# The recurrent mixing layer: where VectorE adds the last batch to X and takes its moments within a step

## What is computed

```python
x = x + 0.5 * L0_ffn(layernorm(x))    # "choice": experts choose tokens
x = x + L0_attn(layernorm(x))         # "rwkv": the layer of this change
x = x + 0.5 * L0_ffn(layernorm(x))    # "choice"
x = x + 0.5 * L1_ffn(layernorm(x))    # "top2"
x = x + L1_attn(layernorm(x))         # "mlstm"
x = x + 0.5 * L1_ffn(layernorm(x))    # "top2"
```

```python
x = _layernorm(x, ln_g, ln_b)
k, v, r = (mix_n(x, last_x) @ W_n.T for n in "kvr")
den = den * td + exp(k)               # per channel, from token to token
num = num * td + exp(k) * v
out = (sigmoid(r) * num / (den + 1e-8)) @ Wo.T
```

## Time and profile before

| | |
|---|---|
| median of 3 runs | 1990.86 us (1990.62 to 1991.52) |
| the profiled execution | 1991.48 us, of which the span of the page is 1989.7 us |
| TensorE, matmuls | busy 1533.6 us (77%) |
| VectorE | busy 1483.6 us (75%) |
| ScalarE | busy 1027.4 us (52%) |
| GpSimd | busy 1048.6 us (53%) |
| the rwkv layer's reciprocals | from 391.5 to 571.4 us of the span |

### The profile page before, as it was taken

One profiled execution on the slowest core, in us unless ns is written; L12 is line 12 of the kernel. 1 busy time (PEld: TensorE's weight loads), 2 busy tenths in 40 slices (PEclk: granted clock), 3 DMA queues, 4 the chain that ended last, 5 costly groups with the idle time before them and its releaser, 6 DMA issues.

```text
span 1989.7 us, 42086 instructions
## 1 busy us (share of the span) xinstructions
PE 1533.6 (77%) x10496; PEld 1430.5 (72%) x10496; DVE 1483.6 (75%) x4465; ACT 1027.4 (52%) x2548; POOL 1048.6 (53%) x1639
## 2 busy tenths in 40 slices
PE   6399999578756999978049995469899978069993
PEld 6299999466645999977049994358888867059993
DVE  6769898688876788888627776658878877447774
ACT  2388888222314888852126663136666642036662
POOL 3527786678852355443644445405666653644442
PEclk9999999798976999996569998559999975579997
DMA  4111010370001111002122223011111100122215
GB/s 169 33 34 37 29 35 9 94 168 0 0 1 49 33 33 34 25 5 107 40 61 67 63 54 88 7 35 64 53 53 63 53 22 23 49 62 67 63 44 170
DMA packets 95551, 104.31 MB, mean 52 GB/s; under 512 B 12328, under 2 KB 75965, under 8 KB 94880
## 3 DMA queue, kind: packets, MB, share of 16 engines
q1 hardware_dynamic: 85472, 85.09, 14.5%
q0 software_dynamic: 9920, 17.35, 2.6%
HBM read 67.94 MB, written 37.97 MB: 53 GB/s over the span
## 4 chain that ended last, share of the span: by engine, by line
PE 53%; DVE 25%; issue 10%; POOL 4%; ACT 2%; DMA 2%; DVEq 1%; SPq 1%; ACTq 0%; POOLq 0%
PE banks L542 5%; PE banks L531 3%; PE banks L522 3%; PE banks L1030 3%; PE banks L524 3%; PE banks L523 3%; PE banks L1043 3%; PE banks L1032 3%; PE banks L1031 3%; DVE rwkv_over L1533 3%; PE banks L1045 3%; PE banks L1044 3%; PE banks L1065 3%; DVE bnstats L241 3%; DVE mlstm_log_decay L1961 2%
## 5 line engine op out<-in xcount | busy, mean ns | idle before, releaser
L809 POOL DMA_INDIRECT rt_y<-top_y,top_xs x182 | 178.7, 982 | 230.0 <-DVE top_y L766 207.5
L1250 DVE TENSOR_TENSOR choice_hlo<-choice_h,choice_hhi 128x512 fp32r<-128x512 f32 x256 | 172.5, 715 | 49.1 <-ACT choice_hhi L1127 48.2
L802 POOL DMA_INDIRECT rt_rows<-top_payload,top_slot x128 | 130.6, 1020 | 110.8 <-DVE top_slot L722 73.6
L1119 ACT ACTIVATE choice_h<-banks 128x512 f32<-128x512 f32 x256 | 152.3, 600 | 61.8 <-PE banks L1032 48.7
L752 DVE SCALAR_TENSOR_TENSOR top_h<-top_silu,top_xs,banks 128x176 f32<-128x176 f32 x364 | 128.5, 394 | 41.4 <-ACT top_silu L596 40.4
L1030 PE MATMUL banks<-choice_xin_hi,ec_w_hi 128*128 128x256 f32 x512 | 146.7, 287 | 6.1 <-ACT choice_xin_lo L1112 4.7
L1043 PE MATMUL banks<-choice_hhi,ec_w_hi 128*128 128x256 f32 x512 | 145.7, 285 | 2.9 <-DVE choice_hlo L1250 2.9
L1127 ACT ACTIVATE choice_hhi<-choice_h 128x512 fp32r<-128x512 f32 x256 | 146.6, 625 | 0.0
L1032 PE MATMUL banks<-choice_xin_hi,ec_w_lo 128*128 128x256 f32 x512 | 144.8, 283 | 0.0
L1031 PE MATMUL banks<-choice_xin_lo,ec_w_hi 128*128 128x256 f32 x512 | 144.7, 283 | 0.0
L1045 PE MATMUL banks<-choice_hhi,ec_w_lo 128*128 128x256 f32 x512 | 143.3, 280 | 0.0
(11 more groups left out here) (303 smaller groups left out, 5676.7 us busy)
## 6 DMA issues: line engine op xcount, KB each, us to landing
choice_token_row<-choice_tokens SPq DMA_DIRECT2D x64, 256.0 KB, 3.1
mlstm_run_row<-mlstm_run SPq DMA_DIRECT2D x32, 512.0 KB, 3.6
rt_rows<-rt_blank SPq DMA_DIRECT2D x2, 6188.0 KB, 35.8
top_xs<-rt_rows SPq DMA_DIRECT2D x182, 68.0 KB, 1.8
top_y_in<-rt_y SPq DMA_DIRECT2D x16, 512.0 KB, 7.2
X<-in_x SPq DMA_DIRECT2D x8, 512.0 KB, 6.8
ec_stage<-in_ec_w SPq DMA_DIRECT2D x2, 2048.0 KB, 15.6
out_x<-X SPq DMA_DIRECT2D x8, 512.0 KB, 7.4
```

The costliest lines, as they stand in the source:

```text
L809: pool.indirect_dma_start(d.y[self.run], bass.IndirectOffsetOnAxis(ap=at, axis=0), self.y[:, u % self.YR, :], None, bounds_check=NT * P - ...
L1250: dve.tensor_tensor(flat(self.hlo), self.h[:, c, :], flat(self.hhi).bitcast(F32), ALU.subtract).then_inc(self.hlo_done, 1)
```

## The change

VectorE's order in a step of the rwkv layer. The addition to X for batch s-1 moves from the end of the step to the place between num and under. The moments for batch s-1 (before: of batch s-2, at the beginning of the step) are parted: the statistics, with their two waits, stand between under and the reciprocal; the aggregation, with its wait, between the reciprocal and z. In step 32, which has no `mix`, addition and moments of batch 31 follow each other. Nothing else is touched: the same instructions on the same tiles and buffers, the same semaphores and counts.

```diff
+    def stats_of(self, dve, layer, b, u):
+        if inside(b):
+            n = layer * B + b
+            apart(dve, self.sh.x_done, n - B + 1, self.sh.passed)
+            self.spread(dve, n, 1, b, slice(0, TP), u)
+
+    def gather_of(self, dve, layer, b, u):
+        if inside(b):
+            self.gather(dve, layer * B + b, 1, slice(0, TP), u)
+
...
     def take(self, dve, n, count, b, tiles, u):
-
+        self.spread(dve, n, count, b, tiles, u)
+        self.gather(dve, n, count, tiles, u)
+
+    def spread(self, dve, n, count, b, tiles, u):
         apart(dve, self.scaled, n - count, self.sh.passed)
         for t in range(tiles.stop):
             i = dve.bn_stats(self.st[:, u, t, :], self.sh.X[:, bass.ds(TP * b + t, 1), :])
         i.then_inc(self.stats, count)
+
+    def gather(self, dve, n, count, tiles, u):
         apart(dve, self.stats, n + count, self.sh.passed)
         for t in range(tiles.stop):
             i = dve.bn_aggr(self.mv[:, u, t, :], self.st[:, u, t, :])
...
         def mix(b, u):
+            last = lambda part: part(dve, self.layer + 1, b - 1, 1 - u)
             td = self.td[:, 0:1].to_broadcast([P, T])
...
             dve.tensor_tensor_scan(self.num[:, u, :], td, self.ekv[:, u, :], 0.0, ALU.mult, ALU.add).then_inc(self.scans_done, 1)
+            if inside(b - 1):
+                update(b - 1, 1 - u)
             dve.wait_ge(self.scans_done, b + 1)
             dve.wait_ge(self.er1_done, b + 1)
 
             dve.scalar_tensor_tensor(out=self.under[:, u, :], in0=self.den[:, u, :], scalar=1e-8, in1=self.er1[:, u, :],
                                      op0=ALU.add, op1=ALU.mult).then_inc(self.under_done, 1)
+            last(sh.moments.stats_of)
             dve.wait_ge(self.under_done, b + 1)
             dve.reciprocal(self.over[:, u, :], self.under[:, u, :]).then_inc(self.over_done, 1)
+            last(sh.moments.gather_of)
             dve.wait_ge(self.over_done, b + 1)
...
         def step(s, u):
-            self.moments_next(dve, s - 2, u)
             if inside(s):
                 mix(s, u)
-            if inside(s - 1):
+            if isinstance(s, int) and s == B:
                 update(s - 1, 1 - u)
+                sh.moments.moments_of(dve, self.layer + 1, s - 1, 1 - u)
```

## The result

| | before | changed |
|---|---|---|
| median, same chip | 1991.19 us (1990.62 to 1991.95, 4 runs) | **1973.82 us** (1972.25 to 1974.71, 4 runs) |
| ratio | 1 | 0.9912 (95% interval 0.9895 to 0.9929) |
| the profiled execution, its span | 1991.48, 1989.7 us | 1972.25, 1970.5 us |
| first to last reciprocal of the rwkv layer | 391.5 to 571.4, 180.0 us | 390.8 to 553.7, 162.9 us |
| step in the hardware loop (mean of 23) | 5.86 us | 5.33 us |

The change saves 17.4 us, 0.88%; 12.6 were forecast.

The account below looks back on a forecast made before the run. VectorE was taken to bound the rwkv layer, at 5.86 us a step. Savings of 9.4 (loop), 3.2 (other steps) and 1.2 (end), less 0.7 (first interval) and 0.5 (TensorE), gave 12.6 us: 1978.3 us, range 1968 to 1989.8.

Parts of the forecast that it names:

- VectorE sets the step: In the rwkv layer the chain runs through VectorE nearly throughout; a step takes 5.86 us, 0.70 of it idle.
- VectorE's own step, 4.85 us: VectorE's new step in the rwkv loop with nothing else in its way: 4.85 us, 1.01 below the kernel before.
- rival (a): GpSimd keeps losing 1.01 to 1.1 us a step at other places, VectorE waits for 1 + exp(-r); 1988.9 us, chance 0.16.
- Rival (b): No VectorE instruction can start early; a step is the plain sum of durations, 5.83 us with num's loss; 1989.8, chance 0.05.
- X's wait for TensorE, costed at nothing: The moved addition needs TensorE's product of the last batch; ekv, den and num stand between, so it costs nothing.
- The timetable with GpSimd: Both engines laid side by side, colliding on SBUF: num loses 0.35 us, z 0.08; both rounds come to 5.4.
- 5.45 taken for the step: Step in the loop with collisions: 5.45 us for 5.86, bounds 5.15 to 5.80; 23 steps save 9.4 us.
- The seven steps outside the loop: The seven other intervals between reciprocals, after the first, fall from 5.8 to about 5.35 us, saving 3.2 us.
- rival (c): The collisions between VectorE and GpSimd mostly vanish: step 5.0 us, 26.0 us saved, 1964.9 us; chance 0.10.
- TensorE's low-clock spells, 0.5 us: Spells at 1.2 GHz delay the projection ahead of X's product, 0.3 us in one step of four; 0.5 lost in all.
- The ends: The layer's first interval gets X and moments, 0.7 us longer; at its end 1.2 us are won.
- Rival (d): Slower: GpSimd holds VectorE's den, num, under and z for more than 1.01 us a step; at 1.3, 1999.4 us; chance 0.08.

Follow-up runs that it names:

- before_act: The kernel before, with GpSimd's scaling of rwkv_xn run on ScalarE as two activations; 1.0013 times the kernel before.
- before_psum: The kernel before, with ekv written over v in PSUM, so num has one input in SBUF; 1.0009 times the kernel before.
- after_act: The changed kernel, with GpSimd's scaling of rwkv_xn run on ScalarE; 0.9871 times the kernel before.
- x_early: The changed kernel, with the addition to X right behind ekv, ahead of both scans; 1.0065 times the kernel before.
- after_again: The changed kernel once more, no edit, on the chip of the variants; 0.9911 times the kernel before, step 5.44 us.
- x_only: The kernel before, with only the addition to X moved between num and under, moments left in place; 0.9957 times the kernel before.
- joined: The changed kernel, with the aggregation straight behind the statistics, both ahead of the reciprocal; 0.9931 times the kernel before.

## Why the prediction was right, step by step

**VectorE sets the step.** Right, and now shown for the kernel before: before_act and before_psum take work or waiting from GpSimd and gain nothing. For the changed kernel the prediction had both engines at 5.4 us, and that is what the profile shows, 5.33 with neither idle for another engine, and GpSimd's own round at 4.6 (forecast 4.67). Their rounds are coupled there, through the collisions and through 1 + exp(-r), and no run says that one alone sets the step. Once GpSimd has 0.6 us a step to spare (after_act), VectorE does.

**VectorE's own step, 4.85 us.** Right. The rest in the table is 4.86 for the changed kernel and 4.78 in its second profile, and 4.74 to 4.77 where GpSimd is less in the way. Both of its sources are measured: 0.48 us of idle time is gone, and 0.5 of gaps between instructions that depend on each other (5.37 to 4.86). Of the 4.86, some 0.06 is under waiting for 1 + exp(-r): it starts 0.38 behind X at 458.20, just behind the end of that instruction at 458.09, where the written-out steps show 0.31 to 0.32. That is all that is seen of rival (a). Rival (b), that a step is the plain sum of durations, gives 5.83 with num's loss, and is out by half a microsecond. The Trainium skill (VectorE: DVE Perf Modes, The DRAIN you can't avoid) speaks for (b) where it says that leaving out semaphores saves nothing; here putting an independent instruction behind one that others wait for did save, 0.5 us over a step. Its remark that an instruction that isn't held starts earlier is what the timeline shows: den starts 0.34 behind ekv, which is 0.41 long.

**X's wait for TensorE, costed at nothing.** Right: no idle time ahead of X in the loop. x_early shows how near the edge it is: two scans earlier the wait is 0.70 us a step.

**The timetable with GpSimd.** Right in the profiled execution, term by term: num held 0.36 (forecast 0.35), 1 + exp(-r) 0.77 (0.76), den 0.06 and z 0.03 (0.18 for both and the statistics), power back at 0.71. The mean was to be held by under for 0.2; it slips through at 0.19, and the small instruction behind it is held instead (0.35). But after_again shows other terms and a loss of 0.66 instead of 0.47, and the forecast's 0.53 lies between them. The order of service, num behind the waiting scaling, was taken from one case in rows 10; it holds in each of the 23 steps (num 1.03), and the 5.65 of the other order is out. The sum was well judged; that the single terms agree so closely is partly chance. The rule behind it (the Trainium skill, SBUF — State Buffer, Who interferes with whom: two SBUF inputs of VectorE against a GpSimd instruction that reads SBUF) agrees with the runs: num with one input in PSUM is held by nothing, 0.66 us.

**5.45 taken for the step.** 5.33 and 5.44 in the two executions, so that the 23 steps save 12.1 us in one and 9.6 in the other, where 9.4 were forecast. Of the 0.12 too much in the first, 0.05 is the caution on top of the timetable's 5.4, and the rest the losses of den, z and the statistics, set at 0.18 and found at 0.09.

**The seven steps outside the loop, "to about 5.35".** This is the term that was mis-sized: 5.6 us were won (6.2 in after_again) and 3.2 expected, less 0.5 for TensorE. The prediction gave these steps the loop's collisions. Two steps of the changed kernel's start:

```profile
399.08 0.67 DVE L1542 TENSOR_TENSOR_SCAN rwkv_num<-rwkv_decay_exp,rwkv_ekv 128x256 f32<-128x256 f32 x1
...
413.74 0.42 DVE L1539 TENSOR_TENSOR rwkv_ekv<-banks,rwkv_ek 128x256 f32<-128x256 f32 x1 [0.97 <-ACT rwkv_ek L1512]
```

num takes 0.67 us in six of the seven. In the last two steps GpSimd has no batch of this layer left to normalize, and the scaling that holds num in the loop isn't there; in the first ones it has less to do for the next layer and stands elsewhere. num is at 1.03 from the step behind the 0.97 us of the second row on. That this wait sets the loop's alignment isn't shown: after_again has no such wait, and num is held there too, at 0.82 and from one step earlier on. The intervals are 4.82, 4.86, 4.87, 5.81, 5.29, 4.72 and 4.69. That is rival (c), step 5.0 and below, in a part of the layer. For the last two steps the kernel's own ranges would have told it: step s normalizes batch s+2.

**TensorE's low-clock spells, 0.5 us.** The size is about right by luck; the event is another. The prediction had a spell delay the product ahead of X, in one step of four; in the loop there is no such wait at all, at a granted clock of 1.00. But outside it, in the interval of 5.81 us, VectorE waits 0.97 for exp(k), while three of the projection's pairs of matmuls take 1.06 us each instead of 0.59 and the granted clock of the interval is 0.80, so partly at 1.2 GHz. The kernel before had 6.08 instead of 5.7 us at the same place (0.85), so some 0.6 more is lost there, inside the 5.6 above. By its last sign, VectorE waiting ahead of ekv, the prediction would be wrong altogether; one such wait in the 31 intervals doesn't decide that.

**The ends.** The first interval grew by 0.70 (0.7); the end won 1.4 (1.2), with the last scaling at +7.29 (+7.47).

**Rival (d), slower.** Not this order. x_early is 0.65% slower than the kernel before, with 1.43 us a step of idle time and collisions against the 1.01 from which the prediction let it decide; but the rival speaks of collisions alone, and they are 0.68 of it.

Summed: forecast 9.4 + 3.2 - 0.7 + 1.2 - 0.5 = 12.6; found 12.1 + 5.6 (with TensorE's share in it) - 0.7 + 1.4 = 18.4, and 0.7 of chance; by the medians it is 17.4. The mechanism was right. Of the 5.8 us between 12.6 and 18.4, 2.7 are the step's length, 2.9 the steps outside the loop and 0.2 the end. The second profile shows what of that is a matter of the alignment: there the loop saves 9.6, and only the steps outside it, with 6.2, stay well above the forecast.

## What to carry to other kernels

Where one engine sets the time, put independent work of it between a result and its use, and put the consumer of a semaphore behind a long instruction: here that took 1.0 us of gaps and waits out of a 5.9 us step. Then cost the second-order loss before counting the gain: lay the engine's instructions with two SBUF inputs beside GpSimd's. Here 0.5 to 0.7 us of the 1.0 went back that way, on instructions that change from one execution to the next; an operand kept in PSUM takes an instruction out of that game. And cost the steps at both ends of a pipeline by themselves, since the other engines' programs are shorter there.

## What the runs showed of the hardware

- **In these runs a held instruction of VectorE ended a fixed time after GpSimd's.** With 256 columns and two SBUF inputs: z 0.28 us (461.33 to 461.61 in x_only, 462.62 to 462.90 in after_again), under 0.29 (466.88 to 467.17 in x_early); the scans den and num 0.53 to 0.55 in five cases, from both x_early and after_again and from the changed kernel. So in these cases the loss can be read off GpSimd's end alone.
- **A waiting GpSimd instruction is served ahead of VectorE's next one.** The scaling that came during den (456.64) got its inputs before num, which was issued only as den ended. That it is so in every step of the loop is read from num's 1.03 us in all 23.
- **The same program has several alignments.** den, num and z took 0.74, 1.03 and 0.45 us in one execution and 0.87, 0.81 and 0.74 in another. The medians of the runs have the same ratio to the kernel before; the two profiled executions themselves are 4.6 us apart.
- **Small differences by neighbour.** The reciprocal takes 1.753 us behind an instruction that it waits for and 1.735 behind the statistics (1.720 behind the aggregation, in joined); two aggregations take 0.25 us behind the statistics that they wait for and 0.19 behind the reciprocal. Why isn't settled.
